# The V products of a burst step placed ahead of the step's maximum and score products

## What is computed

```python
# 16 heads of 32; x: (2, 512, 512), ctx: (2, 8192, 384)
q = (layernorm(x) @ Wq + bq).reshape(B, N, 16, 32)
k = (ctx @ Wk + bk).reshape(B, M, 16, 32)
v = (ctx @ Wv + bv).reshape(B, M, 16, 32)
scores = einsum('bnhd,bmhd->bhnm', q, k) / sqrt(32)
out = einsum('bhnm,bmhd->bnhd', softmax(scores), v)
x = x + relu(out @ W1 + b1) @ W2 + b2
# ... mixer, ffn, quantised ffn with LoRA follow
```

## Time and profile before

| what | us |
|---|---|
| median of 3 runs (3169.69 to 3173.9) | 3171.7 |
| the profiled execution | 3170.58 |
| its span | 3168.5 |
| PE busy in the span | 3045.8 (96%) |
| DVE busy | 2268.5 (72%) |
| POOL busy | 1930.1 (61%) |
| ACT busy | 1697.6 (54%) |

### The profile page before, as it was taken

How to read it: one execution, slowest core, us unless ns; L and a number is a source line. 1 busy time by engine, 2 the same in 40 slices (tenths; PEclk the granted TensorE clock), 3 DMA queues, 4 the chain that set the end, 5 groups by cost and what they waited for, 6 DMA issues and landing times.

```text
span 3168.5 us, 41413 instructions
## 1 busy us (share of the span) xinstructions
PE 3045.8 (96%) x15408; PEld 1833.7 (58%) x15408; DVE 2268.5 (72%) x3635; ACT 1697.6 (54%) x2967; POOL 1930.1 (61%) x487
## 2 busy tenths in 40 slices
PE   7999999999999999999999999999999877899999
PEld 4666666666666666666666666666534332344477
DVE  7777777777777777777777777777747799995653
ACT  2566666666666666666666666666641455330021
POOL 1688888988888888988888888888850000000000
PEclk9999999999999999999999999999999888899999
DMA  5422222222223233232223222232131112124100
GB/s 151 127 51 71 72 75 61 61 74 72 71 51 79 68 94 91 61 83 64 71 51 87 60 71 61 71 82 55 46 141 38 41 66 94 53 80 160 67 14 17
DMA packets 100683, 230.13 MB, mean 73 GB/s; under 512 B 22850, under 2 KB 27970, under 8 KB 99234
## 3 DMA queue, kind: packets, MB, share of 16 engines
q1 hardware_dynamic: 100484, 227.49, 26.3%
HBM read 114.46 MB, written 8.06 MB: 39 GB/s over the span
## 4 chain that ended last, share of the span: by engine, by line
PE 82%; DVE 14%; issue 1%; ACT 1%; POOL 1%; DMA 0%; SPq 0%; ACTq 0%; DVEq 0%; POOLq 0%
PE ps L1777 15%; PE ps L1738 15%; PE ps L1764 12%; PE ps L1691 9%; PE ps L1722 9%; DVE pm L997 7%; PE ps L1715 6%; PE ps L1978 4%; PE ps L1942 3%; PE ps L1789 3%; PE ps L1958 2%; DVE bx L1238 1%; PE ps L1750 1%; PE ps L1746 1%; POOL psum L854 1%
## 5 line engine op out<-in xcount | busy, mean ns | idle before, releaser
L997 DVE TENSOR_REDUCE pm<-ps 128x1 f32<-128x512 f32 x2048 | 1406.4, 691 | 623.6 <-PE ps L1738 549.2
L1462 ACT ACTIVATE pf<-ps 128x512 f32<-128x512 f32 x2048 | 1217.3, 601 | 776.7 <-PE ps L1764 700.7
L854 POOL TENSOR_TENSOR psum<-psum,pf 128x2048 f32<-128x2048 f32 x254 | 1167.1, 4595 | 139.2 <-ACT pf L1462 127.8
L1738 PE MATMUL ps<-ks,qs 96*128 96x512 f32 x2048 | 854.2, 417 | 26.9 <-DVE pm L997 24.7
L1764 PE MATMUL ps<-qs,ks 98*128 98x512 f32 x2048 | 814.3, 399 | 2.1 <-ACT pf L1462 1.9
L854 POOL TENSOR_TENSOR psum<-pf 128x2048 f32<-128x2048 f32 x127 | 581.4, 4578 | 183.0 <-ACT pf L1462 183.0
L1738 PEld LDWEIGHTS ps<-ks,qs 96*128 96x128 f32 x2048 | 387.0, 189 | 319.5 <-issue 213.2
L1777 PE MATMUL ps<-pf,V 128*32 128x512 f32 x4096 | 493.9, 600 | 0.0
L1764 PEld LDWEIGHTS ps<-qs,ks 98*128 98x128 f32 x2048 | 390.7, 191 | 49.6 <-ACT pf L1462 11.3
L863 POOL PARTITION_ALL_REDUCE qstat<-qstat x2 | 0.7, 366 | 630.3 <-DVE qstat L1274 630.3
L1715 PE MATMUL ps<-cTh,Wkg 128*128 128x512 f32 x732 | 292.7, 400 | 3.0 <-ACT V L1451 0.4
(11 more groups left out here) (214 smaller groups left out, 3100.8 us busy)
## 6 DMA issues: line engine op xcount, KB each, us to landing
ks<-KH SPq DMA_DIRECT2D x512, 128.0 KB, 2.4
ks<-KL SPq DMA_DIRECT2D x256, 128.0 KB, 2.4
cT<-in_ctxT SPq DMA_DIRECT2D x32, 768.0 KB, 4.6
Wkg<-wk_rows SPq DMA_DIRECT2D x61, 384.0 KB, 3.0
BC<-bc_rows SPq DMA_DIRECT2D x32, 512.0 KB, 4.8
ring<-in_ffn_w SPq DMA_DIRECT2D x16, 1024.0 KB, 5.4
wA<-in_W_fcT SPq DMA_DIRECT2D x4, 1024.0 KB, 10.1
wB<-in_W_projT SPq DMA_DIRECT2D x4, 1024.0 KB, 7.0
```

The costliest lines, as they stand in the source:

```text
L854: pool.tensor_tensor(acc, before, pf[:, tile % P_SLOTS, :], ALU.add).then_inc(s_sum, 1)
L997: dve.tensor_reduce(pm[:, n // BLK, n % BLK:n % BLK + 1], src, AX.X, ALU.max).then_inc(s_wfree, 1)
L1462: act.activation(pf[:, tile % P_SLOTS, j * NTOK:(j + 1) * NTOK], ps[:, S_BANK + u % S_BANKS, :], ACT.Exp, scale=SCALE).then_inc(s_exp, 1)
L1738: last = pe.matmul(dst, qs[0:3 * HD, h, t * P:(t + 1) * P], ks[0:3 * HD, keys_of(of, j), i * 512:(i + 1) * 512], start=True, stop=True)
```

## The change

In the PE list, the call of `burst` moves from behind the step's A, S and M to the head of the step. Nothing else changes: the lists of DVE, ACT, POOL and SP are the same before and after.

```diff
             for i in range(STEPS):
                 if i == TURNED:
                     ...
+                if i > 0 and i % (BURST * HG) == 0 and i // (BURST * HG) - 1 <= BURSTS:
+                    burst(i // (BURST * HG) - 1)
                 if i + SB_AHEAD < UNITS:
                     for x in work_at(i):
                         if x[0] == "A":
                             fill(x)
                     scores(i + SB_AHEAD)
                 for x in work_at(i):
                     if x[0] != "A":
                         fill(x)
-                if i > 0 and i % (BURST * HG) == 0 and i // (BURST * HG) - 1 <= BURSTS:
-                    burst(i // (BURST * HG) - 1)
                 if side_at(i):
                     fill_side(*side_at(i))
```

## The result

| | us |
|---|---|
| before, median of 4 runs | 3172.5 |
| changed, median of 4 runs (3429.6 to 3430.9) | 3430.7 |
| ratio, 95% interval | 1.0814 [1.0796, 1.0833] |

The page of the changed kernel: the span, the busy times, and the groups with their idle time, which answer.

What follows compares the result with a forecast made beforehand. PE, busy 96% of the span, bounds the kernel, so new PE waits add to the end. 117.1 + 62.0 + 79.9 + 9 - 10.8 = 257.2 us on 3170.6 gives 3427.8, forecast as 3429 us; range 3377 to 3481.

Steps and rivals of the forecast that it cites:

- V to K, step 16: K piece waits for ACT's copy to V, behind the exponential, in step 16: 0.96 us, 61 times.
- V to K, step 32, with casts, less the old waits: Same K piece wait at step 32: 0.96 us, 61 times, plus 9 us for casts, less 10.8 for present waits.
- K to V, step 8: V piece waits for DVE's KL, behind the maximum, in step 8: 1.00 us, 62 times, 62.0 us.
- Points 1 to 3: Late side-bank hand-overs, counted from e, the start of A after the burst: 117.1 (V to K), 62.0 and 79.9 us.
- Point 3: K to V at step 24, M between: V piece waits for KL until e + 2.45; 1.31 us, 61 times, 79.9 us.
- Point 4: ACT's three context casts behind a V copy delay the next exponentials: 0.6 us, 15 times, 9 us, bounds 0 and 15.
- Point 5: In 30 places the copy to V already waited for the burst; that 0.36 us each goes away: -10.8 us.
- Point 6: Costed at nothing: burst start behind a side piece (26 us either way), waits for M's rows, key copies, POOL's adds.
- Only the K hand-overs: Rival: copy to V gets done beside the burst, so points 1, 4, 5 vanish: 3314 us; chance 0.06.
- Follow-on waits: Rival: each of 246 hand-overs is followed by another wait of 0.36 us, adding 89 us: 3518; chance 0.06.
- the clock: Rival: PE's frequent stops lower the granted clock for a tenth of the loop, adding 130 us: 3559; chance 0.05.
- Faster: Rival: burst frees V 0.5 us earlier, hand-overs are not late, only point 5 is left: 3161 us; chance 0.02.

Runs made afterwards that it cites:

- split_s: Kernel before, but a burst step issues A, M, burst, S, so that only S stands behind the burst; 3292.4 us.
- only_16: Kernel before, with the burst first only in step 16 of each group; 3229.0 us.
- split_a: Kernel before, but a burst step issues S, burst, A, M, so that only A and M stand behind the burst; 3402.8 us.
- hybrid_64: Kernel before, but in steps that are multiples of 64 the burst stands first and ACT's copy to V ahead of the exponential; 3165.0 us.
- max_16: Kernel before with A_AHEAD 4 larger (UPG + 13 for UPG + 9); 3308.1 us.
- both_first: Changed kernel with ACT's copy to V ahead of the exponential and DVE's KL ahead of the maximum of the same step; 3234.0 us.

## Why the prediction was right

**The sum.** 3429 was forecast and 3430.7 measured; 257.2 us of change against 258.2. Its terms, beside the group difference of each single-place kernel times its count:

| term | predicted | measured |
|---|---|---|
| V to K, step 16 | 58.6 | 0.96 x 61 = 58.6 |
| V to K, step 32, with casts, less the old waits | 56.8 | 0.82 x 61 = 50.0 |
| K to V, step 8 | 62.0 | 1.01 x 62 = 62.6 |
| K to V, step 24 | 79.9 | 1.39 x 61 = 84.8 |

**Points 1 to 3** hold to 0.01 us: the waiting pieces come at e + 1.91, 1.94 and 2.45 where 1.90, 1.94 and 2.45 were worked out, and the waits are counted 123 and 123 times (122 and 123). DVE frees the bank 0.05 us after KL's end (1019.25 + 0.74 to 1020.04), as taken from ACT's.

**Point 3** was sized 0.08 us a group too low. M took 0.20 in both orders of my sum. Between S and the burst it costs only 0.11: in the kernel before the burst starts 0.44 after S where M lies between, and 0.33 where it doesn't. Behind the burst it costs its full 0.20. So moving it costs 0.09 x 61 = 5 us.

**Point 4** was too high: in the groups with casts the stretch is 9.10 and not 8.87, 0.23 us in place of 0.6, 3.5 us in place of 9. The errors of points 3 and 4 have opposite signs and nearly the same size, so that the total came within 1 us is luck; the parts are good to some 7 us each.

**Point 5** holds: without casts, 8.24 us became 8.87 in the groups with the old wait (+ 0.63; 0.60 forecast) and 7.90 became 8.87 in the others (+ 0.97; 0.96).

**Point 6** holds in its largest unknown: the burst starts 0.21 after a V piece that itself takes 0.12, and 0.33 after a K piece that takes 0.23, so 0.09 to 0.10 more than its spacing, the same as behind S. PE had one wait for the rows of M in all (1.0 us). The restart of 0.10 us is real in all three places (1010.29 to 1010.62, and for a V piece 0.22 in place of 0.12), so the row was the right guide, and not the rule of weight loads pulled ahead from the Trainium skill (TensorE: Matmul & The Clock Gate, Part 2: What happens when you issue a matmul): the load at 1010.28 waits with its matmul.

**The rivals.** "Only the K hand-overs" is out by split_s and only_16. "Follow-on waits" and "the clock" are out for this kernel, but both appeared in its neighbours: 0.1 to 0.24 us at a burst, less than the 0.36 put on them, and 1.5 us in split_a for a stretch that lost the clock. "Faster" named waits that are worth 11 us by the sum; hybrid_64 gained 7.8.

## What to carry to other kernels

- A long burst on the critical engine is cover for the others. Before moving it, list what each other engine must finish before the first waiting instruction behind it, in that engine's own order: here the copy that frees the bank stood behind an instruction fed by the moved product. The price is then a sum of start-to-start times read off rows of the old kernel; here the time from the burst's end to each waiting piece came out right to 0.01 us.
- Moving the producer and not the consumer's order made 258 us; the same PE order with the consumers' two copies first costs 62. An order is a property of all the lists together.
- Test a sum place by place. Four kernels that changed one of four places each added up to the whole within 2 us, which shuts out any cause that depends on how many places are changed. A cause that costs the same at each place needs its size, or a kernel that moves one of the instructions alone, to be told apart.

## What the runs showed of the hardware

**DVE held by POOL.** I had not expected max_16's result. A DVE instruction with two SBUF inputs (L1031) waits inside its recorded duration until POOL's running add ends: 2778 ns as median against 174. The reduction just ahead of it with one input (L1030, 0.19 us) ran beside the same POOL instruction. The Trainium skill (SBUF — State Buffer, 🔬 SBUF: two separate sides) says that DVE and POOL share one port pair as an exclusive lock, held for a whole instruction, and that a DVE instruction takes it in a 2-port mode or, against a POOL instruction that reads SBUF, with two SBUF inputs; the trace agrees for L1031. Two inputs are not the only case: once in max_16, L1031 slipped in just ahead of an add, and L1032 behind it, which has one input, was held until the add ended.

```profile
1209.88 0.17 DVE L1031 TENSOR_TENSOR mn<-mc,m_run 128x16 f32<-128x16 f32 x1
1210.09 4.42 DVE L1032 TENSOR_SCALAR nm<-mn 128x16 f32<-128x16 f32 x1
```

In the kernel before, the chain stands where POOL is between two adds or has just ended one. Moving it by 4 units of A_AHEAD cost 135 us through this hold and, in 17 groups, through the clock that fell behind it. How the 86 us of these 17 groups divide between a longer hold and the clock is an estimate; no kernel of its own separates them.

**The clock near its edge.** In the changed kernel, with a stop of 0.86 to 1.21 us at each burst (PE busy 92% of the loop), the granted clock stayed at 1.00. In split_a, with 0.67 and 0.43 us of idle time within 1.5 us behind a burst, it fell for some 3 us in 12 of 61 groups. In max_16 it held behind idle times of 1.3 us and fell behind those of 3.1.

**A wait that costs without being late.** In both_first an A whose release comes just as its turn comes starts on time (1028.64), but the S behind it comes 0.33 later and not 0.23. Its weight load starts 0.01 us before it, where loads in the stream start beside the matmul ahead (1028.17 for the K piece at 1028.40). That this load is what costs the 0.10 us is read from the rows and was not tested.
